# First feed-forward stage of a fused eight-stage kernel: routing weights applied before the down products instead of after them

## What is computed

```python
def _L0_ffn_ref(x, Wr, router_bias, Wg, Wu, Wd, conv_w, conv_b):   # x: (4096, 128), layer-normed
    scores = sigmoid(x @ Wr)                                       # 8 experts
    _, idx = top_k(scores + router_bias, 2)
    w = take(scores, idx); w = w / (sum(w) + 1e-9)
    cw = zeros(T, 8).at[rows, idx].add(w)
    g, u = einsum('th,ehi->tei', x, Wg), einsum('th,ehi->tei', x, Wu)   # 4 experts with an MLP, i = 64
    hid = silu(g) * u
    mlp_out = einsum('tei,eih->teh', hid, Wd)
    routed = einsum('te,teh->th', cw[:, :4], mlp_out)
    routed = routed + cw[:, 4:5]*x + cw[:, 6:7]*x + cw[:, 7:8]*relu(x)
    return routed + depthwise_conv(x, conv_w, taps=4) + conv_b
x = x + tanh(g_ffn[0]) * _L0_ffn_ref(_layernorm(x), ...)
```

## Time and profile before

| | |
|---|---|
| median of three runs | 1773.29 us (1773.21 to 1775.44) |
| profiled execution: span from the first to the last instruction | 1745.3 us |
| profiled execution: its own whole time | not listed beside the span; the median is 28.0 us above the span |
| PE / DVE / ACT / POOL busy over the span | 1438.7 / 1186.8 / 1029.4 / 528.2 us |
| stage F0, first statistics to last x added | 315.2 to 460.7 us |

### The profile page before, as it was taken

How to read it: one execution, slowest core, us unless ns; L and a number is a source line. 1 busy time by engine, 2 the same in 40 slices (tenths; PEclk the granted TensorE clock), 3 DMA queues, 4 the chain that set the end, 5 groups by cost and what they waited for, 6 DMA issues and landing times.

```text
span 1745.3 us, 35805 instructions
## 1 busy us (share of the span) xinstructions
PE 1438.7 (82%) x9936; PEld 1035.9 (59%) x9940; DVE 1186.8 (68%) x3868; ACT 1029.4 (59%) x3064; POOL 528.2 (30%) x553
## 2 busy tenths in 40 slices
PE   3767777788779997699799998999997329999995
PEld 3445555566454444444356666666666229999995
DVE  2888888588676656588446776677677346666665
ACT  2777787433245555422277777777776227777773
POOL 4453347212111101300000134124313345555451
PEclk9998999899899998799899999999999659999998
DMA  7000019800059980000000001001000612222226
GB/s 181 19 7 6 6 33 165 118 0 0 13 98 165 164 111 25 25 1 0 0 7 8 11 23 33 16 17 32 20 10 23 241 46 62 66 66 65 67 64 241
DMA packets 143563, 98.44 MB, mean 56 GB/s; under 512 B 20610, under 2 KB 132652, under 8 KB 142292
## 3 DMA queue, kind: packets, MB, share of 16 engines
q1 hardware_dynamic: 134740, 80.15, 24.1%
q0 software_dynamic: 8704, 16.87, 2.9%
HBM read 43.10 MB, written 54.93 MB: 56 GB/s over the span
## 4 chain that ended last, share of the span: by engine, by line
PE 37%; issue 32%; DVE 14%; ACT 8%; POOL 4%; DMA 2%; SPq 1%; DVEq 1%; POOLq 0%; ACTq 0%
PE bank L1318 6%; PE bank L1326 6%; PE bank L926 5%; ACT att L1482 3%; PE bank L942 3%; PE bank L975 3%; ACT arena L1359 2%; PE bank L962 2%; DVE nm L1837 2%; PE bank L952 2%; POOL dispatched_rows L702 2%; PE bank L930 2%; DVE att L1838 1%; DVE tmp L2115 1%; DVE arena L1981 1%
## 5 line engine op out<-in xcount | busy, mean ns | idle before, releaser
L1359 ACT ACTIVATE arena<-bank 128x512 f32<-128x512 f32 (+6 forms) x460 | 260.7, 598 | 124.4 <-PE bank L1247 56.2
L1482 ACT ACTIVATE att<-bank,arena 128x128 f32<-128x128 f32 x512 | 181.4, 376 | 81.1 <-DVE arena L1981 79.4
L558 POOL TENSOR_TENSOR rstd<-ve,mhalf 128x4 f32<-128x4 f32 x64 | 64.8, 1012 | 507.5 <-DVE ve L1818 507.5
L1752 ACT ACTIVATE att<-bank,arena 128x128 f32<-128x128 f32 x576 | 164.5, 370 | 73.3 <-PE bank L1318 73.2
L702 POOL DMA_INDIRECT dispatched_rows<-arena x128 | 132.7, 1037 | 209.4 <-DVE arena L1899 153.1
L753 POOL DMA_INDIRECT expert_outputs<-arena x144 | 143.1, 994 | 146.1 <-DVE arena L2439 131.0
L1359 ACT ACTIVATE xnT<-bank 128x128 f32<-128x128 f32 (+1 forms) x180 | 63.5, 353 | 159.2 <-PE bank L774 98.4
L1326 PE MATMUL bank<-arena,att 128*128 128x128 f32 x1152 | 153.3, 276 | 0.9 <-ACT att L1752 0.3
L1318 PE MATMUL bank<-xnT,arena 128*128 128x128 f32 x1152 | 153.9, 278 | 0.2 <-ACT xnT L1359 0.2
L1326 PEld LDWEIGHTS bank<-arena,att 128*128 128x128 f32 x1152 | 140.2, 192 | 3.0 <-ACT att L1752 3.0
L1318 PEld LDWEIGHTS bank<-xnT,arena 128*128 128x128 f32 x1152 | 141.6, 194 | 0.5 <-ACT xnT L1359 0.5
(11 more groups left out here) (347 smaller groups left out, 3266.3 us busy)
## 6 DMA issues: line engine op xcount, KB each, us to landing
dispatched_rows<-padf SPq DMA_DIRECT2D x16, 2128.5 KB, 34.7
arena<-dispatched_rows SPq DMA_DIRECT2D x144, 64.5 KB
cxT<-in_ctx SPq DMA_DIRECT2D x32, 256.0 KB, 2.8
arena<-in_L_ffn_w SPq DMA_DIRECT2D x8, 1024.0 KB, 13.7
arena<-expert_outputs SPq DMA_DIRECT2D x8, 1024.0 KB, 14.4
expert_outputs<-arena POOLq DMA_INDIRECT x144
dispatched_rows<-arena POOLq DMA_INDIRECT x128
out_x<-x SPq DMA_DIRECT2D x8, 256.0 KB, 4.4
```

Source lines behind the costliest of these rows:

```text
L1359: copy = lambda o, i: nc.scalar.activation(o, i, ACT.Copy)
L1482: last = nc.scalar.activation(ex3_of(w, side)[:, i, :], bank[side][:, i * P:i * P + P], ACT.Exp, bias=nm3[:, w % 2, h:h + 1], accum_out=su ...
L1752: last = nc.scalar.activation(h3[:, s % 2, k * P:k * P + P], bank[s % 2][:, k * P:k * P + P], ACT.Gelu, bias=b1c3[:, s % 4, k:k + 1])
```

## The change

`wd0` loses its zero blocks: a pair of experts now stands one above the other on the partitions, 128 columns wide, so that a product with it sums over both experts. So the routing weights must be in before. ACT spreads the four weights of each token over 64 features each (`wide0`, 128 x 1024); PE transposes that (8 transposes, `spread`) into banks 6 and 7; DVE multiplies it with `hid0` into `scaled0` (2 instructions of 128 x 512); PE's down products of `scaled0` go on top of the convolution in bank 5, as one accumulation opened by one bias product of 512 columns. DVE's 16 instructions are gone, and one `tensor_tensor` adds bank 5 to `tmp`. The two comparisons in the router become one. The two `gate_up` of the next chunk follow each other without the wait for `F0_down_read`.

```diff
@@ -30,7 +30,6 @@
 DRAIN0, DRAIN3 = 8, 3
-DOWN0 = (6, 7, 3, 4)
 E0, I0 = 4, 64
...
 TAPS0 = 4
@@ -209,7 +208,7 @@
         wg0, wu0 = sb("wg0", [P, E0 * I0]), sb("wu0", [P, E0 * I0])
-        wd0 = sb("wd0", [P, 2, 2 * P])
+        wd0 = sb("wd0", [P, 2, P])
         cw0, cb0 = sb("cw0", [P, TAPS0]), sb("cb0", [1, P])
...
         causal = sb("causal", [P, P])
@@ -267,14 +266,14 @@
         up0 = ar([P, 2, W])
-        hid0 = ar([P, 2, W])
+        hid0, scaled0 = ar([P, 2, W]), ar([P, 2, W])
         cin0 = ar([P, CB, TAPS0 - 1 + P])
...
         top0, idx0, idf0 = ar([P, CB, 8]), ar([P, CB, 8], U32), ar([P, CB, 8])
-        oh0 = ar([P, 2, CB, R0])
+        oh0 = ar([P, CB, 2, R0])
         wsum0 = ar([P, CB])
-        cwt0 = ar([P, CB, R0])
+        cwt0, wide0 = ar([P, CB, R0]), ar([P, CB, E0, I0])
         ccp0 = ar([P, CB])
...
         fresh()
@@ -401,9 +400,9 @@
             pair, u = divmod(e, 2)
-            WD.append((wd0[I0 * u:I0 * u + I0, pair, P * u:P * u + P], a["L0_ffn_Wd"][e]))
-        s_first, s_load, s_wd, s_zero = sem("first_loaded"), sem("setup_loaded"), sem("wd0_loaded"), sem("wd0_zeroed")
+            WD.append((wd0[I0 * u:I0 * u + I0, pair, :], a["L0_ffn_Wd"][e]))
+        s_first, s_load, s_wd = sem("first_loaded"), sem("setup_loaded"), sem("wd0_loaded")
         s_const = sem("constants_ready")
...
         GATES, VECTOR, SUMS, SUMS_READ, WEIGHTS = 1, 2, 3, 4, 5
@@ -447,7 +446,6 @@
                     sp.dma_start(dst, src).then_inc(s_load, 16)
-            sp.wait_ge(s_zero, 1)
             for dst, src in WD:
...
@@ -531,8 +529,7 @@
             s_held = sem("held")
-            step(pl.memset(wd0[:, :, :], 0.0))
-            pl.memset(rstd[:, :], 0.0).then_inc(s_zero, 1)
+            step(pl.memset(rstd[:, :], 0.0))
             step(pl.memset(ident[:, :], 0.0))
...
                                   pattern=[[-1, P]], channel_multiplier=1))
@@ -642,8 +639,8 @@
                     pl.wait_ge(sem("F0_silu"), c * 2 + (k + 3))
-                    if k == 0 and not first:
-                        pl.wait_ge(sem("F0_down"), c * CB)
+                    if not first:
+                        pl.wait_ge(sem("F0_scaled"), c * 2 + (k - 1))
                     pl.tensor_tensor(hid0[:, k, :], up0[:, k, :], sg0[:, k, :], ALU.mult).then_inc(sem("F0_hid"), 1)
...
             hidden(0, True)
@@ -1030,29 +1027,41 @@
                 pe.wait_ge(s_xdone, c + (NC * STAGE["F0"] + 1))
+                nc.tensor.matmul(bank[5][:, :], ones[0:1, :], cb0[:, :].unsqueeze(1).to_broadcast([1, CB, P]), start=True, stop=False)
                 for j in range(CB):
                     for k in range(TAPS0):
-                        nc.tensor.matmul(bank[5][:, j * P:j * P + P], cin0[:, j, k:k + P], taps0[:, k, :], start=(k == 0), stop=False)
-                    last = nc.tensor.matmul(bank[5][:, j * P:j * P + P], ones[0:1, :], cb0[:, :], start=False, stop=True)
-                last.then_inc(sem("F0_conv"), 1)
+                        nc.tensor.matmul(bank[5][:, j * P:j * P + P], cin0[:, j, k:k + P], taps0[:, k, :], start=False, stop=False)
+            def spread(c):
+                pe.wait_ge(sem("F0_wide"), c + 1)
+                for k in range(2):
+                    pe.wait_ge(sem("F0_scaled"), c * 2 + (k + 1))
+                    for j in range(CB):
+                        last = nc.tensor.transpose(bank[6 + k][:, j * P:j * P + P],
+                                                   wide0[:, j, 2 * k:2 * k + 2, :].rearrange("p e i -> p (e i)"), ident[:, :])
+                    last.then_inc(sem("F0_spread"), 1)
+            def down(c):
+                for k in range(2):
+                    pe.wait_ge(sem("F0_scaled"), c * 2 + (k + 3))
+                    for j in range(CB):
+                        last = nc.tensor.matmul(bank[5][:, j * P:j * P + P], scaled0[:, k, j * P:j * P + P], wd0[:, k, :],
+                                                start=False, stop=(k == 1 and j == CB - 1))
+                last.then_inc(sem("F0_down"), 1)
...
                 conv(c)
-                pe.wait_ge(sem("F0_hid"), c * 2 + 4)
-                for j in range(CB):
-                    if j == 2 and more:
-                        pe.wait_ge(sem("F0_tanh"), c + 2)
-                        transpose_x("F0", c + 1).then_inc(sem("F0_xT"), 1)
-                    for k in range(2):
-                        last = nc.tensor.matmul(bank[DOWN0[j]][:, k * 2 * P:(k + 1) * 2 * P], hid0[:, k, j * P:j * P + P], wd0[:, k, :],
-                                                start=True, stop=True)
-                    last.then_inc(sem("F0_down"), 1)
+                spread(c)
+                if more:
+                    pe.wait_ge(sem("F0_tanh"), c + 2)
+                    transpose_x("F0", c + 1).then_inc(sem("F0_xT"), 1)
+                down(c)
                 if more:
                     router(c + 1)
-                    gate_up(c + 1, 0)
-                if more:
-                    pe.wait_ge(sem("F0_down_read"), c * CB + CB)
-                    gate_up(c + 1, 1)
+                    for k in range(2):
+                        gate_up(c + 1, k)
...
             pe.wait_ge(sem("F0_constants"), 1)
@@ -1544,6 +1553,10 @@
                     copy(up0[:, k, :], bank[2 + 2 * k][:, :]).then_inc(sem("F0_silu"), 1)
+                act.wait_ge(sem("F0_weights"), c + 2)
+                act.wait_ge(sem("F0_spread"), c * 2 + 2)
+                copy(wide0[:, :, :, :], cwt0[:, :, 0:E0].unsqueeze(3).to_broadcast([P, CB, E0, I0])).then_inc(sem("F0_wide"), 1)
...
                 f0(c)
@@ -2051,6 +2064,8 @@
             dve.sem_inc(sem("F0_hid"), 2)
+            dve.sem_inc(sem("F0_scaled"), 2)
+            dve.sem_inc(sem("F0_spread"), 2)
             dve.sem_inc(sem("F0_weights"), 1)
...
             def f0_stats(c):
@@ -2078,12 +2093,11 @@
                 step(v.tensor_copy(idf0[:, :, :], idx0[:, :, :]))
-                for r in range(2):
-                    step(v.tensor_tensor(oh0[:, r, :, :], iota8[:, 0:R0].unsqueeze(1).to_broadcast([P, CB, R0]),
-                                         idf0[:, :, r:r + 1].to_broadcast([P, CB, R0]), ALU.is_equal))
-                step(v.tensor_tensor(oh0[:, 0, :, :], oh0[:, 0, :, :], oh0[:, 1, :, :], ALU.add))
-                step(v.tensor_tensor(cwt0[:, :, :], oh0[:, 0, :, :], lg0[:, :, :], ALU.mult))
+                step(v.tensor_tensor(oh0[:, :, :, :], iota8[:, 0:R0].unsqueeze(1).unsqueeze(1).to_broadcast([P, CB, 2, R0]),
+                                     idf0[:, :, 0:2].unsqueeze(3).to_broadcast([P, CB, 2, R0]), ALU.is_equal))
+                step(v.tensor_tensor(oh0[:, :, 0, :], oh0[:, :, 0, :], oh0[:, :, 1, :], ALU.add))
+                step(v.tensor_tensor(cwt0[:, :, :], oh0[:, :, 0, :], lg0[:, :, :], ALU.mult))
                 step(v.tensor_reduce(wsum0[:, :], cwt0[:, :, :], AX, ALU.add))
...
                 step(v.reciprocal(wsum0[:, :], wsum0[:, :]))
@@ -2093,6 +2107,12 @@
                     f0_norm(c + 1, False)
+                for k in range(2):
+                    dve.wait_ge(sem("F0_spread"), c * 2 + (k + 3))
+                    dve.wait_ge(sem("F0_hid"), c * 2 + (k + 3))
+                    dve.sem_inc(s_held, 1)
+                    v.tensor_tensor(scaled0[:, k, :], bank[6 + k][:, :], hid0[:, k, :], ALU.mult).then_inc(sem("F0_scaled"), 1)
...
                 dve.wait_ge(sem("F0_xn_kept"), c + 1)
@@ -2104,19 +2124,7 @@
-                for j0 in (0, 2):
-                    dve.wait_ge(sem("F0_down"), c * CB + (j0 + 2))
-                    before = [None, None]
-                    for e in range(E0):
-                        for q in range(2):
-                            j = j0 + q
-                            if e:
-                                step.until(before[q])
-                            before[q] = step.issue(v.scalar_tensor_tensor(tmp[:, j, :], b4(DOWN0[j])[:, e, :], cwt0[:, j, e:e + 1], tmp[:, j, :],
-                                                                          ALU.mult, ALU.add))
-                    step.until(before[1])
-                    dve.sem_inc(sem("F0_down_read"), 2)
-                dve.wait_ge(sem("F0_conv"), c + 1)
+                dve.wait_ge(sem("F0_down"), c + 1)
                 step(v.tensor_tensor(tmp[:, :, :], b4(5), tmp[:, :, :], ALU.add))
...
                 if ahead:
@@ -2129,7 +2137,7 @@
             f0(0, True, True)
-            step.loop(13 + 2 + 2 + CB * E0 + 1)
+            step.loop(12 + 2 + 2 + 1)
             with dve.Fori(1, NC - 2) as c:
...
                 f0(c, True, True)
```

## The result

The changed kernel takes 1741.05 us in the median of four runs (1737.27 to 1741.73), the kernel before 1773.25 beside it (1772.27 to 1775.44): a ratio of 0.982, interval 0.9805 to 0.9835, 32.2 us less. One execution of `a_delay4`, further down, took 1971.73 us at a mean granted clock of 0.729, and its times leave that one out.

The account below looks back on a forecast made before the run. The prediction took DVE's loop as the bound: 8.2 + 1.25 + 4.5 = 13.95 us a chunk, taken as 14.0 against 16.92, saving 20.3 over the chunks: 1773.3 - 20.3 = 1753.0 us, range 1747.5 to 1760.5.

Parts of the forecast that it names:

- DVE's loop as the bound, L2115 on it whole: In F0, DVE's loop sets 16.92 us a chunk; L2115's 4.71 us a chunk lies all on the path.
- Steps 3 and 4: Single router comparison: weights end 8.2 us after L2120 starts; ACT's wide copy: 1.05 us, plus 0.1 hand-over on either side.
- table load: Rival: ACT's table load of 1.28 us falls between weights and wide copy, 15.3 a chunk, 1762; chance 0.13 shared with POOL's.
- Steps 2 and 6: Two scaling multiplications, 1.6 us together; next L2120 start (A) comes 4.5 us after the spread's start (S).
- PE's sum: PE's own work per chunk of F0, added from single durations: 13.6 us, 13.8 with two waits, 0.15 behind DVE's chain.
- PE alone: Rival: router less blocked by POOL, so PE's work sets 13.6 us a chunk, 1750.2 in all; chance 0.17.
- Steps 7 and 8: On PE: 16 narrower down products at 0.135 each, 2.2 us, hidden; single bias product saves 0.74 us, off the chain.
- Step 9: The early memset of `wd0`, 0.52 us, goes; covered by later loads, so no gain, 0.5 us if uncovered.
- The sum over chunks: F0's saving: six loop chunks 17.4 us, chunk 0 2.9, last chunk 0.4, together 20.7, taken as 20.3.
- The seven later stages are untouched and slide forward whole.: Stages after F0 keep their length, so nothing was added to or taken from the forecast for them.
- once more: Rival: POOL blocks DVE a further 1.25 us a chunk, 15.2 a chunk, 1761.4 in all; chance 0.13 shared with table load.
- The low clock: Rival: PE falls to 1.2 GHz in F0, its 13.6 us a chunk becoming about 25, 1830 in all; chance 0.03.

Follow-up runs that it names:

- a_delay4: Changed kernel with one added DVE instruction four times at the end of F0, as a pure delay: 1726.29 us (median of three), ratio 0.9849.
- b_nosum: Kernel before without the 16 DVE instructions of L2115, routed experts' outputs left out of `x`: 1746.86 us, ratio 0.9851.
- a_nopool: Changed kernel without POOL's product `hid0`, the scaling taking `up0` in its place: 1738.99 us, ratio 0.9802.
- b_delay3: Kernel before with three extra DVE instructions ahead of the last sum of F0, nothing taken away: 1749.43 us in 12 runs, ratio 0.9985.
- b_again: Kernel before, unchanged, run and profiled a second time: 1772.2 us, ratio 0.9997.
- a_wide2: Changed kernel with the wide copy made twice, the first time into a spare tile: 1728.65 us, ratio 0.9864.
- a_both: Changed kernel with POOL's product ahead of its power step and the wide copy in two halves: 1718.46 us, ratio 0.9802; run again 1735.27, 0.9803.
- a_bias4: Changed kernel with the bias again as four products of 128 columns in place of one of 512: 1724.59 us, ratio 0.9848.

## Why the prediction was right or wrong

- **DVE's loop as the bound, L2115 on it whole: right.** `b_nosum` gives 18.8 us for it alone, and would have given more if PE had let it.
- **Steps 3 and 4: right.** Weights' end at 8.24 (8.2 forecast), wide copy 1.06 (1.05), spread at 9.46 (9.45). The table load begins behind the copy, off the chain.
- **Steps 2 and 6: too dear by 0.4.** The two multiplications take 1.29 together, not 1.62: they overlap, and the pair in front of L2128 takes 2.07. So the next A stands at S + 4.11, not S + 4.5. The chain is 13.57 where 13.95 was worked out and 14.0 taken. That such a multiplication, with one input in PSUM, is not held up by POOL is borne out by the rows from A0 above. As a rule for every instruction with one SBUF input it was put too widely: in the last chunk of the changed kernel the 128x4 L2102, with one input in SBUF, took 0.95 beside POOL's product, 0.17 without.
- **PE's sum, 13.6 to 13.8: too high by 1.0 to 1.2.** PE's pace where it is the bound is 12.57 (`a_nopool`). From start to start there, the 32 taps take 3.68 (4.3 in the sum), the down products 1.89 (2.2), the gate and up products 3.61 (3.8). The 0.135 of step 7 was read between bias products, and without these a tap takes 3.68 / 32 = 0.115. So PE stood 1.0 behind the chain, not 0.15, and the two loops did not rub. "PE alone" named the pace that came, 13.6, but it came by the chain, so it met the number by luck; PE alone would set 12.6. "PE busy over 95%" came out at 94%.
- **Steps 7 and 8: right that both are off the chain.** The down products start at S + 1.59 and end at S + 3.64; no wait for them stands before L2128. Step 8's 0.74 was too small: the bias in pieces costs PE 1.19, since the taps between the pieces slow down too, and 0.2 of it shows.
- **Step 9: nothing seen.** A0's scatter of 7 us hides 0.5.
- **The sum over chunks: too small at both ends.** Chunk 0 to chunk 6 took 100.53 in the first trace and takes 81.29, 19.2 less where 17.4 was forecast. The time from A0's end to chunk 0's addition fell by 4.1 (2.9 forecast), the last chunk by 2.2 (0.4 forecast: 14.30 is the length of a window that begins behind an addition, the time between the two additions is 14.80; PE was rightly taken to set it, but at 13.8, and it is 12.57). "I take 20.3, since the first turns may be shorter" went the wrong way. In all the stage gave 25.5 in place of 20.3: the terms were of the right kind and 5 us too small. That alone would have ended at 1773.3 - 25.5 = 1747.8, just inside the range.
- **The step that failed in kind: "The seven later stages are untouched and slide forward whole."** It put at nothing what took the result out of the range. They became shorter by 5.8 us: A1 0.4, F1 2.5, A2 1.4, F2 0.7, A3 0.7, end 0.1. A pure delay, `b_delay3`, has 0.4, 2.5, 1.3 and 0.6 of A1, F1, A2 and F2, so at least that much goes by when the stages begin and not by what the change does. In F1 it is a stretch of the low clock that comes or does not come; for A2 and F2 this is likely by the windows at their border, but not shown alone. The rest of 32.2, about 1 us, is within A0's scatter and cannot be told apart.
- **The rivals.** POOL hits as before and not once more: `a_nopool` has 0.5 in the cast and 1.0 in the comparison, in size as before. No table load stands on the chain. The low clock did not come in the steady turns of F0 (1.00); it mattered in the later stages, which the prediction did not look at.

What stays open: what decides where a low stretch falls. The cases alternate with F0's length (114.5 long, 116.6 to 116.8 short, 117.6 long, 119.1 to 120.3 short, 121.8 long, 123.1 to 126.8 short, 145.6 long, 147.6 short), and repeats with A0 of 315.0, 316.6 and 318.9 had the same later stages, so it isn't the time since the start. What the chip goes by wasn't tried further.

## What to carry to other kernels

Close the loop through the engines and price its whole length, then ask which loop stands next and how far behind: here removing 4.71 of VectorE's work was worth 2.7 until PE's work went too. Single durations of neighbouring instructions are not to be added; take the pair or group from start to start. An engine that shows as busy all the time can still be waiting: compare its pace with a run in which the other loop is taken away. A forecast for one stage needs a spread of some 5 us for the stages behind it, and an experiment that shortens a stage is to be read by that stage's length, not by the kernel's; adding a small delay shows how much of a difference is only where things fall.

## What the runs showed of the hardware

- **Later stages depend on when they start.** The extra stretch at 1.2 GHz, 3.4 us between 578 and 586 us of `b_again`, costs F1 some 2.5 us; the windows above show it. Two kernels with the same work in F1 differ by 3 us.
- **One kernel, two sets of chips.** The kernel before takes 1751.09 and 1751.46 on two chips, 1772.98 and 1770.75 on two others. Of this A3 holds 25 us (521 to 546), while "end" is 4 to 8 shorter on the slower ones. VectorE in the last chunks of A3, in the changed kernel on the slower kind:

```profile
1347.84 0.69 DVE L2008 COPY arena<-bank 128x512 f32<-128x512 f32 x1 [6.67 <-PE bank L959]
...
1353.54 0.69 DVE L2008 COPY arena<-bank 128x512 f32<-128x512 f32 x1 [5.01 <-remote]
...
1363.45 0.69 DVE L2024 TENSOR_TENSOR tmp<-bank,bo 128x512 f32<-128x512 f32 x1 [9.22 <-remote]
```

and the same instructions in `a_wide2` on the faster kind (its lines stand two lower):

```profile
1343.56 0.69 DVE L2010 COPY arena<-bank 128x512 f32<-128x512 f32 x1 [5.53 <-PE bank L960]
...
1345.53 0.69 DVE L2010 COPY arena<-bank 128x512 f32<-128x512 f32 x1 [1.28 <-PE bank L960]
...
1348.37 0.69 DVE L2026 TENSOR_TENSOR tmp<-bank,bo 128x512 f32<-128x512 f32 x1 [2.14 <-PE bank L973]
```

The waits of 5.01 and 9.22 have no releaser in the trace ("remote"); the other chip waits 1.28 and 2.14 for PE. Their cause is open. Both kernels pay it alike, and the ratio of `a_both` is the same on either kind: 0.9802 and 0.9803.
- **Two multiplications of 0.69 end 1.29 after the first began**, so the second starts 0.60 after the first, with one input from PSUM.
- **The bias in pieces costs PE more than the pieces' own length.** Four bias products of 128 columns between the taps bring bias and taps of a chunk from 4.73 (1.05 + 3.68, `a_nopool`) to 5.92 (`a_bias4`), start to start.
